# Recurrent stage: silu of z in halves beside the convolution's silus, norm and transposes a segment ahead, output projections and convolutions in halves

## What is computed

```
h = layer_norm(x) * norm_w + norm_b
u, z = split(h @ in_w, 2)
u = silu(conv(u) + conv_b)                    # 4 taps along the sequence
dt_low, B, C = split(u @ xproj_w)
dt = softplus(dt_low @ dtproj_w + dtproj_b)
state = exp(dt * A) * state + (dt * u) * B    # for each of 16 states, along the sequence
y = sum_over_states(state * C) + u * skip_D
x = x + (y * silu(z)) @ out_proj_w
```

## Time and profile before

| | |
|---|---|
| median of three runs | 4773.03 us (4762.74 to 4781.94) |
| profiled execution | 4812.17 us, span 4810.5 us |
| mean granted TensorE clock | 0.930 |
| PE busy | 4110.7 us, 85% of the span |
| VectorE busy | 3197.0 us, 66% |
| POOL busy | 2265.1 us, 47% |
| ScalarE busy | 2001.7 us, 42% |
| the recurrent stage's scans | first starts at 70.9 us, last at 2068.0 us |

### The profile page before, as it was taken

The page is one execution under the profiler, slowest core; times in us unless marked ns, Lnnn a source line. Parts: engine busy times, 40 slices in busy tenths (PEclk is TensorE's granted clock), DMA queues, the critical chain, the costliest instruction groups (busy, mean ns, idle before and its releaser), DMA issues. The chain is left out here.

```text
span 4810.5 us, 50784 instructions
## 1 busy us (share of the span) xinstructions
PE 4110.7 (85%) x16032; PEld 2276.1 (47%) x16032; DVE 3197.0 (66%) x5216; ACT 2001.7 (42%) x3534; POOL 2265.1 (47%) x1928
## 2 busy tenths in 40 slices
PE   7888888888998888759858887999968999966998
PEld 2333333333333333224432336888833444655898
DVE  4999999999999999954466645444445554155433
ACT  5666566656565656432234451111112444222100
POOL 6888888888888888820021112444330111000320
PEclk9999999999999999979768898999977999988899
DMA  4555544554455544510062201000061320000000
GB/s 121 133 134 147 136 139 134 139 140 141 134 136 146 140 133 134 143 43 0 0 122 33 40 11 57 14 26 26 1 155 48 53 52 10 9 16 0 27 20 29
DMA packets 288996, 375.34 MB, mean 78 GB/s; under 512 B 100481, under 2 KB 131516, under 8 KB 288508
## 3 DMA queue, kind: packets, MB, share of 16 engines
q1 hardware_dynamic: 288764, 372.57, 30.4%
HBM read 343.80 MB, written 26.21 MB: 77 GB/s over the span
## 5 line engine op out<-in xcount | busy, mean ns | idle before, releaser
L521 POOL TENSOR_TENSOR arena<-arena 128x512 f32<-128x512 f32 x1024 | 1284.3, 1274 | 260.3 <-DVE psum L764 254.6
L764 DVE TENSOR_TENSOR_SCAN psum<-psum,arena 128x512 f32<-128x512 f32 x1024 | 1280.6, 1251 | 78.7 <-ACT psum L670 78.0
L871 PE MATMUL psum<-arena,base 128*128 128x512 f32 x2048 | 1083.9, 631 | 262.5 <-DVE arena L739 261.5
L670 ACT ACTIVATE psum<-arena 128x512 f32<-128x512 f32 x1024 | 699.5, 689 | 271.5 <-DVE arena L739 252.6
L871 PEld LDWEIGHTS psum<-arena,base 128*128 128x128 f32 x2048 | 348.5, 192 | 921.9 <-DVE arena L739 745.0
L739 DVE TENSOR_TENSOR arena<-psum,arena 128x512 f32<-128x512 f32 x1024 | 691.3, 675 | 0.0
L283 POOL TENSOR_TENSOR rounded<-arena,rounded 128x512 fp32r<-128x512 f32 (+2 forms) x181 | 315.9, 1751 | 791.8 <-DVE rounded L279 791.8
L289 PE MATMUL psum<-rounded 128*128 128x256 f32 (+1 forms) x1728 | 561.6, 325 | 33.1 <-DVE arena L1689 16.2
L290 PE MATMUL psum<-rounded 128*128 128x256 f32 (+1 forms) x1728 | 561.0, 325 | 0.0
L291 PE MATMUL psum<-rounded 128*128 128x256 f32 (+1 forms) x1728 | 560.3, 324 | 0.0
L1158 DVE TENSOR_REDUCE arena<-psum 128x1 f32<-128x512 f32 (+3 forms) x768 | 403.2, 555 | 199.6 <-PE psum L1221 139.1
(11 more groups left out here) (287 smaller groups left out, 5171.7 us busy)
## 6 DMA issues: line engine op xcount, KB each, us to landing
arena<-mb_bc_rows SPq DMA_DIRECT2D x512, 512.0 KB, 4.8
arena<-L_ffn_w SPq DMA_DIRECT2D x34, 512.0 KB, 4.4
arena<-f_parts SPq DMA_DIRECT2D x96, 128.0 KB, 6.5
arena<-l_parts SPq DMA_DIRECT2D x96, 128.0 KB, 6.4
l_v<-arena SPq DMA_DIRECT2D x16, 512.0 KB, 3.6
arena<-l_v SPq DMA_DIRECT2D x32, 256.0 KB, 4.4
f_parts<-arena SPq DMA_DIRECT2D x24, 256.0 KB, 2.4
l_parts<-arena SPq DMA_DIRECT2D x24, 256.0 KB, 2.4
```

The costliest lines, as they stand in the source:

```text
L521: eng.tensor_tensor(drive[:, u % RD, :], dtu[:, g % 2, m, :], bc_sb[:, v % RB, 0, :], ALU.mult)\
L670: eng.activation(ps[:, DECAY + u % ND, :], dt[:, g % 2, m, :], ACT.Exp, scale=a_neg[:, g // 4 % 2, m, n:n + 1]).then_inc(decay_ready, 1)
L764: eng.tensor_tensor_scan(state(u), state(u), drive[:, u % RD, :], first, ALU.mult, ALU.add).then_inc(scanned, 1)
L871: eng.matmul(ps[:, Y + u % 2, :], sh.ident, hc[:, u % RW, :], start=False, stop=n == NS - 1).then_inc(added_up, 1)
```

## The change

The arithmetic is the same. What moves is the place p at which each engine does each part of the front work (f is the next segment, f+1 the one after it, g the running one):

| part | engine | p before | p after |
|---|---|---|---|
| statistics, aggregate, shift of f+1 | VectorE | 50 to 53, 54, 57 | 23 to 26, 27, 31 |
| deviation, normalize f+1 | ScalarE | 55; 58, 60, 62, 63 | 29; 36 to 39 |
| turn | PE | 0, 2 for f | 59, 61 for f+1 |
| rows (copy of the turn) | ScalarE | 3, 5 for f | 62, 63 for f+1 |
| in-projection u; copy | PE; ScalarE | 9, 11, 13, 15; 12, 14, 16, 18 | 1, 3, 5, 7; 4, 6, 8, 10 |
| output projection of g-1 | PE | 4, 6 (whole) | 9 to 12 (halves) |
| its addition to x | VectorE | 8, 10 | 13, 15 |
| convolution | PE | 18, 20, 28, 30 (whole) | 14 to 17, 25 to 28 (halves) |
| silu of u, two groups each | ScalarE | 26, 36 | 22, 34 |
| silu of z | ScalarE | 62, all four groups, for f | 22, 34, two groups each, for g |
| x-projection; its copy | PE; ScalarE | 38; 43 | 37; 42 |
| dt projection; step | PE; ScalarE | 42, 44, 46, 48; 47, 49, 51, 53 | 43, 44, 46, 48; 46, 48, 50, 52 |
| exponential | ScalarE | 48, 50, 52, 54 | 47, 49, 51, 53 |
| in-projection z; copy | PE; ScalarE | 50, 52, 54, 56; 55, 57, 59, 61 | 51, 53, 55, 57; 54, 56, 58, 60 |
| tap diagonals of a new block | POOL | 16, 17, 18, 19 | 14, 15, 20, 21 |

At 22 and 34 ScalarE now takes two silus of u for f and one of z for g between one pair of table loads. Ahead of the loop the silu of z of segment 0 is gone (it comes at 22 and 34 of segment 0), the exponential's table is loaded once behind all four silus of u, and the turn of segment 1 is done there. The core of the diff:

```diff
-        return STEPS * f + 2 * max(f - 2, 0) + step + (2 if f >= 2 and step >= UP else 0)
+        return STEPS * f + 2 * max(f - 2, 0) + step + (2 if f >= 2 and step >= CV else 0)
...
-        def gate_z(f):
-            for m in range(M - 2, M):
+        def gate_z(f, half):
+            for m in (2 * half, 2 * half + 1):
                 wait_taken(eng, use(f, ZP + m))
-            eng.activation(sz[:, f % 2], sz[:, f % 2], ACT.Silu).then_inc(z_ready, 1)
-            exp_tables()
+            rows_z = sz[:, f % 2, 2 * half:2 * half + 2, :]
+            eng.activation(rows_z, rows_z, ACT.Silu).then_inc(z_ready, 1)
...
+            if g == 0 and p in (0, 1):
+                rows(1, p)
+            if p in (22, 34):
+                if f < SEGS:
+                    gate_u(f, (p - 22) // 12)
+                gate_z(g, (p - 22) // 12)
+                exp_tables()
...
-            eng.wait_ge(z_ready, g + 1)
+            eng.wait_ge(z_ready, 2 * g + half + 1)
...
-        def convolve(f, m):
+        def convolve(f, m, part):
...
-            for tap in range(KC):
+            for tap in (2 * part, 2 * part + 1):
...
+            if f + 1 < SEGS and p in (59, 61):
+                turn(f + 1, (p - 59) // 2)
             if f < SEGS:
-                if p in (0, 2):
-                    turn(f, p // 2)
-                elif p in (9, 11, 13, 15):
-                    in_projection(f, 0, (p - 9) // 2)
...
+                if p in (1, 3, 5, 7):
+                    in_projection(f, 0, (p - 1) // 2)
+                elif 14 <= p < 18:
+                    convolve(f, (p - 14) // 2, (p - 14) % 2)
+                elif 25 <= p < 29:
+                    convolve(f, 2 + (p - 25) // 2, (p - 25) % 2)
...
+            if g > 0 and 9 <= p < 13:
+                out_projection(g - 1, (p - 9) // 2, (p - 9) % 2)
```

## The result

The changed kernel takes 4854.2 us (median of four runs, 4849.91 to 4870.95), the kernel before 4777.48 (four runs, 4762.74 to 4787.5): a ratio of 1.017 with a 95% interval of 1.0132 to 1.0207. It is slower, by 77 us where 50 were forecast, and 4854 us lie just above the 4805 to 4850 that the forecast gave for itself.

The account below looks back on a forecast made before the run. The prediction took VectorE's pace to bound the stage; 36.9-4.5-4.9+17.4+5.1 gave +50 us, carried over to 4773+50=4823 us. Its own range was 4805 to 4850; over all cases 4760 to 4858, leaving out the faster rival and a tail above.

Parts of the forecast that it names:

- first scan earlier: Ahead of the loop: the silu of z and its table loads go, so the first scan starts earlier, -4.5 us.
- The rule for a wait at a distance d: ScalarE waiting for PE's work d units back: scan p+1 loses F+t+0.92-(1.72(d-1)-0.09), F PE's time, t its own.
- scan 0: Next segment's first scan, behind turn at 61 and rows at 63: loses 1.6 us after even segments, 1.35 after odd.
- the burst: ScalarE's loads and silus at 22: costs 2.5 us in an even segment, 1.9 in an odd one.
- The silu of 1024: ScalarE's half silu of z: no profile row, taken as 1.05 us between bounds 0.69 and 1.91.
- The weights: Segments 3, 7, 11: the in-projection at p=1 waits 5.8 us for the next block's loads, +17.4 in all.
- No turn stands there now: -4.9: Segment starts: waits at p=4 from TensorE's lower clock, in seven segments, vanish since the turns moved away, -4.9 us.
- none at the gates 33 and 34: A sign that the forecast is right: VectorE shows no idle time at gates 33 and 34.
- Rival 3: Lower clock stays at segment starts and falls on the in-projections: 18 us more, 4841 us; chance 0.10.
- the shift waits no more: VectorE's layer norm shift, moved to 31: the wait inside its 0.77 mean ends, about 0.4 if prompt.
- No change by a part that is paid once: Rival: late part paid once per segment, at step and rows, not in units 48 to 61; +9, 4782 us; chance 0.14.
- Faster by the loads: Rival: table switches are the price, ScalarE's lead hides waits for PE; 38 us less, 4735 us; chance 0.11.

Follow-up runs that it names:

- e1: The changed kernel with the next block's weight loads issued at the end of segments 2, 6 and 10: 4821.81 us, one execution.
- e2: The changed kernel with dt projections, steps, exponentials, z projections and z copies back at their places of before: 4785.9 and 4793.9 us.
- e3: The changed kernel with the copies of the turns at 63 and at 1 of the next segment instead of 62 and 63: 4821.91 us, one execution.
- b1: The kernel before with only z's silu moved, in halves, from 62 to behind u's silus at 26 and 36: 4760.83 us, ratio 0.9947.
- e4: The changed kernel with the edits of e1, e2 and e3 together: 4751.52 us, one execution.
- e7: The changed kernel with e4's and e5's edits, u copies and output-projection additions two units later, first burst at 24, second convolutions at 22 to 25: 4685.29 us, ratio 0.9789.
- e5: The changed kernel with VectorE's norm shift at 31 put between scan and weighing instead of behind the weighing: 4851.02 us, one execution.

## Why the direction was right and the size was not

The sum against the runs, by the change of each segment's length:

| term | forecast us | measured us |
|---|---|---|
| first scan earlier | -4.5 | -5.2 |
| segments 2, 6, 10 | +10.8 | +11.0 |
| segments 4, 8, 12 | +10.8 | +19.9 |
| segments 1, 5, 9, 13 | +5.4 | +7.5 |
| segments 3, 7, 11, with the weights | +26.6 | +30.3 |
| segments 0, 14, 15 | +5.8 | +9.4 |
| the old low clock's waits at p=4 (in 1, 4, 5, 6, 9, 12, 13; 14's 0.62 was left out) | -4.9 | in the rows above |
| sum | +50.0 | +72.9 |

**Steps that held.** The rule for a wait at a distance d came out within a tenth of a microsecond nearly everywhere in segments at full clock: scan 47 idles 0.92 (forecast 0.95, all forecasts with 0.09 for the end), the units behind it 0.15 to 0.18 at a period of 1.98, scan 0 waits 1.54 and 1.27 (1.6 and 1.35), the burst 2.32 and 1.69 (2.5 and 1.9), z's copies 0.39 to 0.43 and 0.59. The silu of 1024 takes 1.049 us, where 1.05 was taken between two bounds. The weights cost segments 3, 7 and 11 a further 7.7, 6.7 and 7.5 us, beyond the odd segments' 128.9, 22 in all against 22.5. e1, e2 and e3 each took out one of these terms: 20.3, 60.4 and 23.0 us, where 21.9, 53 and 20.9 were expected. Low stretches of the clock moved too in these runs, and their share is not separated.

**The step that failed: "No turn stands there now: -4.9".** I took the low clock for a trait of the place at which the turns stood and let it go with them, so that the sum had no low clock left but the one behind the weights. In these runs it follows PE's idle time, mostly behind VectorE's stalls (not behind each: scan 0's 1.27 in segments 2, 6 and 10 leaves it up), and the change makes more of these: waits that the sum put at nothing and that the runs show at some 17.8 us, counted below. The trace of before already says so. At the end of segment 2 VectorE stalls for the silu of z (scan 63, 2.71), PE idles 3.40 us for it, the clock is at 0.50 around there, and the turn starts only at 451.34, where the clock is back at 1.00 (PE's timeline, then a window):

```profile
445.43 3.85 PE L871 MATMUL psum<-arena,base 128*128 128x512 f32 x4 [3.40 <-DVE arena L739]
...
451.34 0.60 PE L796 MATMUL psum<-base,arena 128*128 128x128 f32 x4
```

```profile
450.00:456.80 6.80, 6.34 (x20) 2.63 (x18) 6.80 (x9) 3.44 (x6) 6.64 (x7) 1.00 0.81 238
```

b1 shows it by an edit: its turns stand at 0 and 2 as before, the silu of z is gone from 62, and at no segment's start from segment 1 on is the clock low. At the start of segment 3, with the turn at 442.38:

```profile
442.38 0.60 PE L794 MATMUL psum<-base,arena 128*128 128x128 f32 x4
```

```profile
438.00:446.00 8.00, 6.28 (x17) 2.59 (x17) 8.00 (x11) 2.84 (x5) 7.92 (x7) 1.00 0.61 208
```

Over the loop TensorE was at its low level for 78.7 us before, 143.4 after, 102.4 in e3, 68.2 in e4 and 20.2 in e7. Where it falls on PE work for which ScalarE waits, it costs: scan 5 of segments 1, 5, 9 and 13 waits 1.8 to 1.95 instead of the 0.92 of e3, and the same 0.9 is put on 3, 7 and 11, where the wait for the weights hides it (7x0.9=6.3); segment 0's waits 2.89 instead of 1.24 (1.6), segments 4, 8 and 12 are 2.9 longer than 2, 6 and 10 (8.8), and a gate in 14 adds 1.1: 17.8 us. In segment 4 one sees it behind the burst and ahead of the end, in the windows (clock 0.51) and in what VectorE waits for next:

```profile
642.90:646.30 3.40, 3.40 (x4) 1.50 (x5) 3.40 (x9) 1.87 (x6) 1.97 (x2) 0.51 0.36 125
694.10:697.50 3.40, 3.40 (x5) 1.37 (x5) 3.22 (x4) 1.75 (x4) 3.32 (x3) 0.51 0.50 169
```

```profile
656.91 0.69 DVE L726 TENSOR_TENSOR arena<-psum,arena 128x512 f32<-128x512 f32 x1 [1.26 <-PE psum L877]
...
699.84 1.23 DVE L764 TENSOR_TENSOR_SCAN psum<-psum,arena 128x512 f32<-128x512 f32 x1 [2.08 <-ACT psum L669]
```

Segment 2 has neither wait, nor have 6 and 10, and the forecast's sign "none at the gates 33 and 34" failed here. Rival 3, the low clock staying, was priced at 18, gave the right cause ("VectorE's new stall at p=0 leaves PE idle") and stood beside the forecast as something else that could happen; it happened together with it. That its price fits is in part luck, since its place was right only in part: the start of odd segments, but in 4 and 12 gate 33 and scan 55, and in 8 scan 5 (3.61 instead of 1.24) and gate 33 (0.66). That the start's part in odd segments comes from scan 0's wait is shown by e3; the rest of the 17.8 is read from waits and windows and was not taken out alone. Why it is segments 4, 8 and 12 that have the 8.8 is open: in e3 the same two waits, 1.26 at gate 33 and 2.08 at scan 55, stand in 2, 6 and 10 instead.

**A smaller one: "the shift waits no more".** Its 0.77 mean was read as 0.4 of work and a wait that the new place would end. In before it takes 0.40 in even and 1.21 in odd segments, at its new place 0.87 in each, 0.47 more than the 0.4 that I had taken: 14x0.47=6.6 us. e5 takes it down to 0.15, so the 0.4 was mostly waiting too, and its loop gets 7.0 back. With the clock's 17.8 this is 24.4 of the missing 22.9; the other terms, together, were 1.5 too high.

**The rivals.** No change by a part that is paid once: refuted by e2, whose scan 0 waits as before, and by the sum in e4. Faster by the loads: with 30 fewer of them the changed kernel is 73 us slower in the stage, b1 gains 22.5 there and not 38, and e2's 60.4 alone outweighs that.

## What to carry to other kernels

An engine that works in order has a lead counted in units of the pipeline: for each task that is moved, count the units between the producer's step and the waiting one, and price every distance shorter than the lead by itself, for here such losses added up. A step moved ahead meets waits of its inputs (here a load of weights) that it had been behind, so move the load as well. And do not take a stall's price as its length alone where TensorE's clock falls behind it: what comes next on PE is then longer, and may be late for the next consumer.

## What the runs showed of the hardware

The shift on VectorE reads 128x4 elements twice from SBUF. Beside POOL's product it ends when that product ends. The timelines of VectorE and POOL there, in the kernel after, and of VectorE in e5:

```profile
386.39 0.87 DVE L719 SCALAR_TENSOR_TENSOR arena<-arena 128x4 f32<-128x4 f32 x1
```

```profile
385.97 1.27 POOL L521 TENSOR_TENSOR arena<-arena 128x512 f32<-128x512 f32 x1 [0.44 <-DVE psum L764]
```

```profile
386.40 0.15 DVE L719 SCALAR_TENSOR_TENSOR arena<-arena 128x4 f32<-128x4 f32 x1
```

In the kernel after it ends at 387.26 and POOL's product at 387.24: 0.87 us for what takes 0.15 in e5, where it stands behind the scan and POOL has not begun its next product (that starts at 386.57). In before, at p=57, the same holds: in segment 2 the shift takes 0.40 and ends at 432.26, POOL's product at 432.24; in segment 3 it takes 1.21 and ends at 559.31, POOL's at 559.29.

```profile
558.10 1.21 DVE L719 SCALAR_TENSOR_TENSOR arena<-arena 128x4 f32<-128x4 f32 x1
```

```profile
558.02 1.27 POOL L521 TENSOR_TENSOR arena<-arena 128x512 f32<-128x512 f32 x1
```

So its time is what is left of POOL's product when it starts. The Trainium skill, "GPSIMD Engine Reference", section "1. Specifications", says that POOL shares its SBUF interfaces with VectorE and that they contend when a VectorE instruction has two SBUF inputs. The trace agrees, and shows the price here: the shift waits out POOL's product. The scan and the weighing, which take one input from PSUM, run beside the same products at their usual 1.2 and 0.7 us.
